# Correlation-volume convolution: two pixel blocks in one transpose, the rows frame split in two halves

## What is computed

```python
def _L0_conv_ref(feature, conv_w, conv_b):
    norm = jnp.sqrt(jnp.sum(feature * feature, axis=1, keepdims=True))
    fn = feature / jnp.maximum(norm, 1e-12)
    fp = jnp.pad(fn, ((0, 0), (0, 0), (2, 2), (2, 2)))
    sims = []
    for cc in range(5):
        for r in range(5):
            sims.append(jnp.sum(fp[:, :, r:h + r, cc:w + cc] * fn, axis=1))
    x = jnp.concatenate([feature, jnp.stack(sims, axis=1)], axis=1)
    out = jnp.einsum('bihw,oi->bohw', x, conv_w) + conv_b[None, :, None, None]
    return jax.nn.relu(out)

x = x + _L0_conv_ref(_gn(x), L0_conv_conv_w, L0_conv_conv_b)   # _gn: 32 groups
x = x + _L1_conv_ref(_gn(x), L1_conv_conv_w, L1_conv_conv_b)   # the same with L1's weights
```

## Time and profile before

| | us |
|---|---|
| median of 3 runs | 545.12 |
| lowest, highest | 543.14, 550.11 |
| the profiled execution, its own time | 546.7 |
| its span in the profile | 544.9 |
| mean granted clock of TensorE | 0.98 |

### The profile page before, as it was taken

How to read it: one execution, slowest core, us unless ns; L and a number is a source line. 1 busy time by engine, 2 the same in 40 slices (tenths; PEclk the granted TensorE clock), 3 DMA queues, 4 the chain that set the end, 5 groups by cost and what they waited for, 6 DMA issues and landing times.

```text
span 544.9 us, 7801 instructions
## 1 busy us (share of the span) xinstructions
PE 500.3 (92%) x2888; PEld 284.2 (52%) x2888; DVE 352.4 (65%) x820; ACT 285.8 (52%) x386; POOL 132.3 (24%) x189
## 2 busy tenths in 40 slices
PE   0659789599989999999999999999999999999996
PEld 0535455354645646464646556464646455464442
DVE  5788795868777296848667685858676676423322
ACT  1352544585474656647393847556473938433222
POOL 4553520230620313131120403040313122040400
PEclk9988898989998999999999999999999999999999
DMA  8171445350322716583957625041332425362332
GB/s 308 81 270 54 123 182 171 98 158 14 101 70 85 216 42 207 173 293 114 318 173 269 185 97 163 13 128 43 95 88 73 111 83 179 135 202 88 123 124 117
DMA packets 57188, 75.82 MB, mean 139 GB/s; under 512 B 11220, under 2 KB 45068, under 8 KB 57150
## 3 DMA queue, kind: packets, MB, share of 16 engines
q1 hardware_dynamic: 47358, 66.40, 36.3%
q0 software_dynamic: 9792, 8.92, 7.0%
HBM read 34.97 MB, written 37.79 MB: 134 GB/s over the span
## 4 chain that ended last, share of the span: by engine, by line
PE 78%; DVE 12%; ACT 4%; DMA 2%; issue 2%; POOL 1%; SPq 0%; DVEq 0%; ACTq 0%
PE conv_ps L519 55%; PE gram_ps L460 15%; PE conv_ps L528 4%; DVE stats L749 3%; PE turn_ps L509 2%; DVE opnd L798 2%; DVE xs L876 2%; ACT opnd L616 2%; POOL v L422 1%; DMA xs<-in_x_dram 1%; ACT v L622 1%; DVE wmax L848 1%; ACT act_out L652 1%; DMA skew<-band_dram 1%; DVE wl L864 1%
## 5 line engine op out<-in xcount | busy, mean ns | idle before, releaser
L519 PE MATMUL conv_ps<-opnd,wh 128*128 128x512 f16 x512 | 195.3, 381 | 1.4 <-DVE wl L864 1.4
L519 PE MATMUL conv_ps<-opnd,wl 128*128 128x512 f16 x512 | 195.2, 381 | 0.0
L519 PE MATMUL conv_ps<-opnd,whh 128*128 128x512 f16 x512 | 195.0, 381 | 0.0
L652 ACT ACTIVATE act_out<-conv_ps,bias,wdown 128x512 f32<-128x512 f32 x128 | 96.3, 773 | 142.1 <-PE conv_ps L528 128.3
L876 DVE TENSOR_TENSOR xs<-xs,act_out 128x512 f32<-128x512 f32 x128 | 87.6, 695 | 58.0 <-ACT act_out L652 57.5
L460 PE MATMUL gram_ps<-opnd 128*128 128x256 f16 (+1 forms) x960 | 106.3, 270 | 3.4 <-ACT band L632 3.4
L798 DVE SCALAR_TENSOR_TENSOR opnd<-opnd,v 128x1024 f16<-128x1024 f16 x64 | 79.4, 1250 | 36.1 <-ACT v L622 28.9
L460 PEld LDWEIGHTS gram_ps<-opnd 128*128 128x128 f16 x960 | 91.5, 100 | 17.4 <-ACT band L632 4.3
L616 ACT ACTIVATE opnd<-xs,affine 128x1024 f16<-128x1024 f32 x64 | 78.7, 1235 | 17.2 <-DVE affine L792 17.2
L749 DVE BATCH_NORM_STATS2 stats<-xs 128x6 f32<-128x512 f32 x128 | 79.8, 679 | 5.5 <-DMA xs<-in_x_dram 5.4
L519 PEld LDWEIGHTS conv_ps<-opnd,whh 128*128 128x128 f16 x512 | 50.1, 98 | 61.4 <-issue 1.6
(11 more groups left out here) (77 smaller groups left out, 267.8 us busy)
## 6 DMA issues: line engine op xcount, KB each, us to landing
xs<-in_x_dram SPq DMA_DIRECT2D x32, 512.0 KB, 6.6
band_dram<-band SPq DMA_DIRECT2D x64, 256.0 KB, 2.7
out_dram<-xs SPq DMA_DIRECT2D x32, 512.0 KB, 3.1
skew<-band_dram SPq DMA_DIRECT2D x16, 532.0 KB, 4.1
vol<-corr_h POOLq DMA_DIRECT2D x48, 50.0 KB, 2.8
rows_dram<-rows SPq DMA_DIRECT2D x16, 131.6 KB
rows_dram<-rows SPq DMA_DIRECT2D x16, 126.6 KB
mirror<-rows_dram POOLq DMA_DIRECT2D x14, 110.9 KB, 2.5
```

Source lines behind the costliest of these rows:

```text
L519: pe.matmul(conv_ps[:, g % 4, :], w[:, l, t, m * P:(m + 1) * P], opnd[:, u % RING, part, t, n * HALF:(n + 1) * HALF], start=(t == 0 and w ...
L652: act.activation(act_out[:, g % 2, :], conv_ps[:, g % 4, :], ACT.Relu, bias=bias[:, l, m:m + 1], scale=wdown[:, l, m:m + 1]).then_inc(relu, 1)
```

## The change

Two blocks, j and j + 4, stand side by side in `nbr`, 64 values apart, and one transpose turns both: 4 transposes of 115 columns instead of 8 of 52. Block j comes out on partitions 0 to 50, block j + 4 on partitions 64 to 114, all in bank 0 of `turn_ps`. `rows` becomes 115 partitions by a half image of 16 rows with its frame (20 x 36 = 720 values); ACT copies it with one instruction instead of two. The write of rows to DRAM becomes four transfers, two for each half, of the same bytes in all. The read of `skew` becomes two transfers of four blocks each. The group average gets bank 1 of `turn_ps` for its own, and the waits of `average` and `turn` change with it: `average` waits for the copy of the average before it, `turn` for ACT's copy of the rows before it. The memsets of `rows` and of the unused values of `nbr` change in size. Views, correlation and convolution are as they were.

```diff
+    NROWS = BACK + NS
+    HALVES = 2
+    FOLD = BLOCKS // HALVES
+    H_PART = 64
+    FRAME = (HI // HALVES + 2 * R) * PW
+    HALF_PSZ = PSZ // HALVES
-        nbr = sb("nbr", [P, BLOCKS, NROWS], F32)
-        rows = sb("rows", [NROWS, PSZ], F32)
+        nbr = sb("nbr", [P, BLOCKS, H_PART], F32)
+        rows = sb("rows", [H_PART + NROWS, FRAME], F32)
@@ band_through_dram
-                src = bass.AP(band_dram, q * GSZ + GPAD - R, [[BAND + 1, P], [P * BAND, BLOCKS], [1, REACH]])
-                sp.dma_start(skew[:, :, :], src).then_inc(skew_in, 16)
+                for h in range(HALVES):
+                    src = bass.AP(band_dram, q * GSZ + GPAD - R + h * FOLD * P * BAND,
+                                  [[BAND + 1, P], [P * BAND, FOLD], [1, REACH]])
+                    sp.dma_start(skew[:, h:BLOCKS:HALVES, :], src).then_inc(skew_in, 16)
@@ rows_to_dram
-                sp.dma_start(bass.AP(rows_dram, base, [[PSZ, NS + 1], [1, PSZ]]), rows[0:NS + 1, :]
-                             ).then_inc(rows_out, 16)
-                sp.dma_start(bass.AP(rows_dram, base + (NS + 1) * PSZ, [[A_PITCH, S], [B_PITCH, S], [1, PSZ]]),
-                             rows[BACK:BACK + NS, :]).then_inc(rows_out, 16)
+                for h in range(HALVES):
+                    top = base + h * HALF_PSZ
+                    at, n = h * H_PART, slice(h * (FRAME - HALF_PSZ), h * (FRAME - HALF_PSZ) + HALF_PSZ)
+                    sp.dma_start(bass.AP(rows_dram, top, [[PSZ, NS + 1], [1, HALF_PSZ]]),
+                                 rows[at:at + NS + 1, n]).then_inc(rows_out, 16)
+                    sp.dma_start(bass.AP(rows_dram, top + (NS + 1) * PSZ, [[A_PITCH, S], [B_PITCH, S], [1, HALF_PSZ]]),
+                                 rows[at + BACK:at + NROWS, n]).then_inc(rows_out, 16)
@@ average
-                if u > 1:
-                    pe.wait_ge(rows_a, 2 * (u - 1))
-                pe.matmul(turn_ps[:, 0, 0:2 * KT], avg[:, :], mv[:, :, :].rearrange("p t s -> p (t s)"),
+                if u > 0:
+                    pe.wait_ge(gn_step, GN_STEPS * (u - 1) + 1)
+                pe.matmul(turn_ps[:, 1, 0:2 * KT], avg[:, :], mv[:, :, :].rearrange("p t s -> p (t s)"),
@@ turn
-                pe.wait_ge(gn_step, GN_STEPS * min(u + 1, UNITS - 1) + 1)
-                for j in range(BLOCKS):
-                    last = pe.transpose(turn_ps[0:NROWS, j * P // HALF, j * P % HALF:j * P % HALF + P],
-                                        nbr[:, j, :], ident[:, :])
+                wait(pe, rows_a, u)
+                both = nbr[:, :, :].rearrange("p (i h) n -> p i (h n)", h=HALVES)
+                for i in range(FOLD):
+                    last = pe.transpose(turn_ps[0:H_PART + NROWS, 0, i * P:(i + 1) * P],
+                                        both[:, i, 0:H_PART + NROWS], ident[:, :])
@@ rows_out_of_psum
-                for h in range(2):
-                    act.activation(framed(rows[:, :])[:, R + h * SPAN:R + (h + 1) * SPAN, R:R + WI],
-                                   image(turn_ps[0:NROWS, h, :]), ACT.Copy).then_inc(rows_a, 1)
+                act.activation(framed(rows[:, :])[:, R:R + HI // HALVES, R:R + WI],
+                               image(turn_ps[0:H_PART + NROWS, 0, :]), ACT.Copy).then_inc(rows_a, 1)
```

More of the change, by code:

```diff
@@ L77, in build @@
     BACK = NS + 1
-    NROWS = BACK + NS + 1
+    NROWS = BACK + NS
[4 more added lines that the diff above has]
+    HALF_PSZ = PSZ // HALVES
     QUARTERS = 4
@@ L253, in views_from_dram @@
         def views_from_dram(eng, k):
-            eng.wait_ge(rows_out, 32 * (k + 1))
+            eng.wait_ge(rows_out, 64 * (k + 1))
             wait(eng, corr_step, CORR_STEPS * k)
@@ L337, in band_through_dram @@
                 wait(sp, rn_step, RN_STEPS * k)
-                src = bass.AP(band_dram, q * GSZ + GPAD - R, [[BAND + 1, P], [P * BAND, BLOCKS], [1, REACH]])
-                sp.dma_start(skew[:, :, :], src).then_inc(skew_in, 16)
+                for h in range(HALVES):
+                    src = bass.AP(band_dram, q * GSZ + GPAD - R + h * FOLD * P * BAND,
+                                  [[BAND + 1, P], [P * BAND, FOLD], [1, REACH]])
+                    sp.dma_start(skew[:, h:BLOCKS:HALVES, :], src).then_inc(skew_in, 16)
             def rows_to_dram(k):
-                sp.wait_ge(rows_a, 2 * (k + 1))
+                sp.wait_ge(rows_a, k + 1)
                 wait(sp, corr_step, CORR_STEPS * (k - 1))
                 base = k % 2 * ROWS_SZ
-                sp.dma_start(bass.AP(rows_dram, base, [[PSZ, NS + 1], [1, PSZ]]), rows[0:NS + 1, :]
-                             ).then_inc(rows_out, 16)
-                sp.dma_start(bass.AP(rows_dram, base + (NS + 1) * PSZ, [[A_PITCH, S], [B_PITCH, S], [1, PSZ]]),
-                             rows[BACK:BACK + NS, :]).then_inc(rows_out, 16)
+                for h in range(HALVES):
[5 more added lines that the diff above has]
+                                 rows[at + BACK:at + NROWS, n]).then_inc(rows_out, 16)
             load(0)
@@ L400, in _ @@
             pool.memset(wvol[:, :, :], 0.0).then_inc(const_step, 1)
-            pool.memset(nbr[:, :, NROWS - 1:NROWS], 0.0).then_inc(const_step, 1)
+            pool.memset(nbr[:, :, NROWS:H_PART], 0.0).then_inc(const_step, 1)
             def scaled_weights(l):
@@ L641, in rows_out_of_psum @@
                 act.wait_ge(turned, u + 1)
-                wait(act, rows_out, 32 * u)
-                for h in range(2):
-                    act.activation(framed(rows[:, :])[:, R + h * SPAN:R + (h + 1) * SPAN, R:R + WI],
-                                   image(turn_ps[0:NROWS, h, :]), ACT.Copy).then_inc(rows_a, 1)
+                wait(act, rows_out, 64 * u)
+                act.activation(framed(rows[:, :])[:, R:R + HI // HALVES, R:R + WI],
+                               image(turn_ps[0:H_PART + NROWS, 0, :]), ACT.Copy).then_inc(rows_a, 1)
             def rectified(u, g):
@@ L767, in unit_affine @@
                 dve.wait_ge(group_avg, u + 1)
-                dve.tensor_copy(gmv[:, :, :].rearrange("p t s -> p (t s)"), turn_ps[:, 0, 0:2 * KT]
+                dve.tensor_copy(gmv[:, :, :].rearrange("p t s -> p (t s)"), turn_ps[:, 1, 0:2 * KT]
                                 ).then_inc(gn_step, 1)
@@ L820, in neighbours @@
                 base = RN_STEPS * k
-                dve.wait_ge(skew_in, 16 * (k + 1))
+                dve.wait_ge(skew_in, 32 * (k + 1))
                 dve.tensor_scalar(nsq[:, :], skew[:, :, CENTRE], (V_SCALE * 1e-12) ** 2, None, ALU.max
@@ L836, in neighbours @@
                 sk, n = skew[:, :, :], nbr[:, :, :]
-                scale = bass.AP(n.tensor, n.offset + RN_ROW, [list(n.ap[0]), [NROWS, BLOCKS], [0, S], [0, S]])
+                scale = bass.AP(n.tensor, n.offset + RN_ROW, [list(n.ap[0]), [H_PART, BLOCKS], [0, S], [0, S]])
                 for at, first, step_ in ((0, 0, 1), (BACK, REACH - 1, -1)):
@@ L840, in neighbours @@
                                   [list(sk.ap[0]), [REACH, BLOCKS], [step_, S], [step_ * WI, S]])
-                    dst = bass.AP(n.tensor, n.offset + at, [list(n.ap[0]), [NROWS, BLOCKS], [S, S], [1, S]])
+                    dst = bass.AP(n.tensor, n.offset + at, [list(n.ap[0]), [H_PART, BLOCKS], [S, S], [1, S]])
                     dve.tensor_tensor(dst, src, scale, ALU.mult).then_inc(rn_step, 1)
```

## The result

| | before | after |
|---|---|---|
| median, us | 547.16 (4 runs) | 540.04 (4 runs) |
| lowest, highest | 543.14, 550.11 | 539.55, 541.54 |
| span of the profiled execution | 544.9 | 538.4 |
| mean granted clock of TensorE | 0.98 | 0.98 |

The time ratio is 0.989, with a 95% interval of 0.986 to 0.992: 1.1% faster, which is within 2%. The prediction was 540.2 us, from 537.0 to 544.5.

A forecast was written before the change was run, and what follows sets the result against it. PE was taken as the bound from 110 us on, with transfers counting before that. Turns -5.6 and start-up +0.7 gave -4.9 us, put on the median of 545.1: 540.2 us, range 537.0 to 544.5.

The forecast's parts named there:

- The turn, -0.43 a unit: Transposes on PE: four wide ones take 0.44 us instead of 0.87 for eight, 5.6 us over thirteen turns.
- The upper bound: Turn on PE: four wide transposes at 0.21 us each take 0.84, a gain of only 0.03 a unit.
- The start-up, +0.7: Work before the steady part: extra issues on SP's queue cost +0.2 to +1.9 us, taken as +0.7.
- The second skew issue, +0.4: Skew read in unit 2's start-up: its second issue and a gap add 0.4 us to the chain.
- Turn 0: First turn on PE, at low clock: four fewer transposes give 0.96 us, 0.48 left after the clock, then lost.
- The cover: Steady slots: the volume lands 8.7 us before PE needs it, so rows +0.1 to +1.0 us later are hidden.
- The last slot: Last slot: volume lands by 521.0, needed at 522.9, so 1.9 us of cover; lateness beyond that is paid once.
- the sum: Whole kernel: -5.6 for the turns and +0.7 for the start-up make -4.9 us, a gain of 0.9%.
- Wide transposes that cost 0.21: Rival on PE: wide f32 loads at 0.21 us each set the pace, no gain, 545.4 us; chance 0.06.
- durations that add up: Rival on PE: each transpose costs its full 281 ns, so -14.6 + 0.7, 531 us; chance 0.02.
- Each transfer paid to its landing: Rival on the transfers: added landings run one behind another, +11.8 us, 557; chance of any such delay 0.06.
- nothing is lost in the start-up: Rival on the start-up: turn 0's gain stays and SP's delay is hidden, -5.6 - 0.5, 539.0 us; chance 0.15.

The follow-up runs named there:

- the repeat: Kernel before or changed kernel, each unchanged, profiled and timed once more: before 545.33 us, ratio 0.9986; after 539.28 us, ratio 0.987.
- extra transfers: Changed kernel with eight more rows transfers to a spare tensor from unit 3 on: 569.2 us; same with image loads behind the rows: 567.3 us.
- three neighbours of it: Kernel before with only the change's transfers (1.0025); changed kernel with unit 3's transposes issued twice (0.9905); kernel before with unit-1 views on POOL (0.9962).
- turn twice: Changed kernel with each of its four transposes issued twice in every unit: 546.75 us, ratio 1.0.
- split only: Kernel before with only the change's transfers, rows written as four half transfers and skew read as two: 547.94 us, ratio 1.0025.
- twice in unit 3: Changed kernel with the transposes of unit 3 alone issued twice: 540.88 us, ratio 0.9905.
- twice in unit 3, loads late: Changed kernel with unit 3's transposes issued twice and SP's image loads issued behind the rows write: 540.6 us, ratio 0.9893.
- its two later forms: Changed kernel with unit-1 views on POOL plus image loads behind the rows: 538.38 us; then also skew read as one transfer: 537.18 us.

## Why the prediction was right, by its steps

**The turn, -0.43 a unit.** Right. The row for the turning of the weights, four transposes of 128 columns in 0.44 us, gave the cost of the new form exactly. The upper bound, 0.21 us by the load of the average's matrix, did not hold, though the new load has a duration of 178 ns: like the 272 ns of the transpose, it is a duration and no cost.

**The start-up, +0.7.** Not shown. The first pair of profiles gives +0.8, and +0.6 from the first average, but the same start-up moved by 2.8 us from profile to profile, so that this agreement is luck. What can be checked is the terms. The issues cost 1.28 and not 1.10, since the third is 0.45 and not 0.33. The landing, which I left as it was, became about 0.55 shorter, by splitting alone, since the kernel before with split transfers has it too (1.98 us in units 9 and 10). Against the start of the turn the first view came 0.25 us later in a steady slot (6.32 us in unit 10, 6.07 before), where I had said 0.1, and in unit 1 not later but sooner (5.39, where it was 5.95, and 5.57 in the repeat). The second skew issue, +0.4, costs nothing, since the landing behind it shrinks by as much.

**Turn 0.** In the first profile of the changed kernel the average of unit 2 was 1.7 us earlier than before, more than the 0.48 expected, but for a reason of its own: there the granted clock at this turn was 1.0 (2.4 GHz), and in the repeat 0.5 (1.2 GHz), as before. The first rows are of the first profile, the last two of the repeat:

```profile
41.85 0.69 PE L520 MATMUL turn_ps<-ident,nbr 128*115 128x128 f32 x4 [3.51 <-DVE nbr L852]
42.38 0.38 PE L530 MATMUL conv_ps<-opnd,wh 128*128 128x512 f16 x1
```

```profile
41.99 1.13 PE L520 MATMUL turn_ps<-ident,nbr 128*115 128x128 f32 x4 [2.07 <-DVE nbr L852]
42.91 0.63 PE L530 MATMUL conv_ps<-opnd,wh 128*128 128x512 f16 x1
```

With the low clock the four take 0.92 us to the next matmul, near the 0.96 of the prediction, and from the first average to that of unit 2 it is 47.10 us, against 46.42 in the repeat of before: nothing was won. What was won in the first profile was lost in the wait for the volume. The length of the low clock behind that wait is not the change's either: it ends at 65.3 us in the first profile of before and at 67.5 in the first of after, but at 67.5 too in the repeat of before.

**The cover.** 8.7 us in a steady slot was a little too much, since I followed the volume alone. The slots with extra transfers show that DVE's line sets it, at some 7 us of lateness. And I took it for all slots. In slot 4 the rows stand behind an image load and land about 7 us late, and the cover was all but used up already: 2 us more of DVE's wait cost 2.2. The change did not trip it; three neighbours of it did. This is the step of the argument that was weakest, and by luck it had no price in the profiled executions.

**The last slot.** Right. The volume was issued by 511.77 and, at 2.7 us, landed by 514.5 and was asked for at 516.41: 1.9 us of cover, as predicted, and 1.7 by the kernel with extra transfers.

**What the sum lacked.** The prediction read the chain from 110 us on as almost wholly PE work. From 138 to 163 us it was not, and behind that stretch stands the piece near 164 us, 1.7. In the profile before, PE waits 2.0 us there for `wl`, and the 12 matmuls behind it take 4.28, most of them at a granted clock of 0.5 (1.2 GHz, from 164.3 to 167.6 us); after, with the same wait, they take 2.59 at 1.0 (2.4 GHz). In all profiles but those with extra transfers:

| kernel | transposes in unit 3 | turn 3 | piece, us |
|---|---|---|---|
| before, and again | 8 | 131.63, 130.55 | 4.28, 4.28 |
| after, and again | 4 | 132.40, 131.95 | 2.59, 2.59 |
| turn twice | 8 | 132.37 | 4.28 |
| split only | 8 | 133.18 | 4.28 |
| twice in unit 3 | 8 | 130.59 | 3.91 |
| before, unit-1 views on POOL | 8 | 129.51 | 2.59 |
| twice in unit 3, loads late | 8 | 129.18 | 2.59 |
| unit-1 views on POOL, and its two later forms | 4 | 128.45, 131.39, 129.70 | 2.59 |

With four transposes it never fell unless the wait itself was longer (2.84 and 2.40 us in the two kernels with extra transfers, where it did). With eight it fell in five profiles of seven. Neither the turn's length nor its place alone decides, and what does is open. The 1.7 us are thus a real part of the gain of 6.5 in the span, but perhaps no property of the change. The medians give 7.1 us, the ratio of 0.989 gives 6.0, and the medians of the two repeats differ by 6.0. The predicted 4.9 and the piece make 6.6.

**The number.** That 540.04 lies 0.2 us from 540.2 is in part luck: the gain was put at 4.9 and is 6 to 7, and the median of before, on which I put it, was 545.12 of three runs and is 547.16 of four. Times of the kernel before spread wider than those of the changed one (542.48 to 550.13 over the 25 runs beside the repeats, 538.05 to 541.54 over 8). No execution of the kernel before above 547 us was profiled, so what makes these long is open.

**The rivals.** Wide transposes that cost 0.21, and durations that add up, are refuted by 0.44 us for four. Each transfer paid to its landing is refuted too: landings came sooner, not later. The Trainium skill, "DMA: Bandwidth & Descriptors", section "Anatomy of one DMA — SWDGE (gpsimd) path", has a fixed cost of about 2.0 us for a transfer issued by GpSimd; the rows are issued by SP. This case shows: the landing behind the end of the last of four issues was 1.98 us in a steady slot, and 2.55 behind the last of two, so whatever each transfer costs was overlapped and not added. That nothing is lost in the start-up is neither shown nor refuted.

**The best version.** The changed kernel with the views and volume of unit 1 issued in the slot loop: 536.94 us, ratio 0.9825, with one skew transfer and late loads 0.9824. Against the changed kernel run again the first is 0.4% faster. The profile gave 3.5 us in turn 3 (128.45 against 131.95), of which a part is the spread of the start-up; the medians give 2.3.

## What to carry to other kernels

In a dense row an f32 transpose costs by its count and not by how many columns its load has, at least up to 128: pack what is narrow into one wide transpose, and take its price from the spacing of any such row that the trace already has, not from its duration. Cover is to be read in every slot with a different set of transfers in front, not in one steady slot; look above all for small transfers that stand beside a large load. Before a term of a few tenths is read from two profiles, profile the same start-up again: here it moved by 2.8 us with nothing changed. And where the start-up is bound by one issuing queue, move work off that queue before counting tenths of a microsecond in it.

## What the hardware showed that I had not expected

- A load of 115 f32 columns takes 178 ns and the transpose 272, yet they follow one another at 0.11 us.
- Splitting a transfer made it land sooner behind its last issue: 1.98 us for half rows in steady slots and 2.55 for whole ones, 1.70 against 2.26 in unit 0. In issue time the split cost 1.28 us. The second short issue costs 0.45 where the first costs 0.33.
- In slot 4 of the kernels without extra transfers, POOL's first view started 6.4 to 8.0 us behind the start of the last rows issue where a 2 MB load was issued right ahead of the rows, and 2.7 where it was issued behind them. But then the views themselves took 9.6 to 10.1 us and not 6.2 to 8.0.
- After one and the same 2.0 us wait of PE the clock was sometimes low for 12 matmuls (4.28 us) and sometimes not (2.59), the same way again in both repeated kernels.
